# A token tile of the down product behind every second gate or up product, in the first feed-forward of a two-layer model

## The reference

```
xn      = layernorm(x)                                    # 2048 tokens x 512
w_gu    = fp4_values(gate_up_packed) * scales             # 2816 x 512, a scale per 128 inputs
w_down  = fp4_values(down_packed) * scales                # 512 x 1408, a scale per 128 inputs
gate,up = split(xn @ w_gu.T)                              # 1408 columns each
h       = silu(gate) * up
y       = h @ w_down.T
x       = x + tanh(g_ffn[0]) * y / sqrt(mean(y*y) + eps)
```

## Time and profile before

| | |
|---|---|
| median of three runs | 2760.99 us |
| the profiled execution, its own time | 2759.97 us |
| its span | 2757.9 us |
| PE busy | 2507.7 us (91%) |
| DVE busy | 1779.6 us (65%) |
| ACT busy | 1390.4 us (50%) |
| POOL busy | 1033.5 us (37%) |
| 508 to 862 us: PE, DVE, ACT, POOL busy | 316.8, 272.0, 202.5, 190.6 of 354 us |
| granted clock of PE over the span | 0.961 of full speed |

### The profile page before, as it was taken

The page is one execution under the profiler, slowest core; times in us unless marked ns, Lnnn a source line. Parts: engine busy times, 40 slices in busy tenths (PEclk is TensorE's granted clock), DMA queues, the critical chain, the costliest instruction groups (busy, mean ns, idle before and its releaser), DMA issues. The chain is left out here.

```text
span 2757.9 us, 46086 instructions
## 1 busy us (share of the span) xinstructions
PE 2507.7 (91%) x15884; PEld 1965.6 (71%) x15884; DVE 1779.6 (65%) x3774; ACT 1390.4 (50%) x3499; POOL 1033.5 (37%) x965
## 2 busy tenths in 40 slices
PE   7899997699997999998999999999999997299994
PEld 4666664467765788886888888888888886155552
DVE  6767698687876666665766666666667664622221
ACT  4777876455654444443655555555555553022221
POOL 3344321455554555554322222222222221055552
PEclk9999999899998999998999999999999998599997
DMA  3110121200103555557512522331141127599997
GB/s 138 50 47 22 44 65 49 86 1 31 54 31 117 196 181 185 198 178 249 163 47 65 158 74 63 113 97 43 55 151 52 44 78 240 165 301 298 298 297 164
DMA packets 220906, 337.05 MB, mean 122 GB/s; under 512 B 23556, under 2 KB 104836, under 8 KB 220164
## 3 DMA queue, kind: packets, MB, share of 16 engines
q1 hardware_dynamic: 203363, 290.70, 33.2%
q0 software_dynamic: 14912, 39.85, 6.3%
q10 hardware_dynamic: 2400, 3.55, 0.4%
HBM read 227.70 MB, written 110.53 MB: 123 GB/s over the span
## 5 line engine op out<-in xcount | busy, mean ns | idle before, releaser
L2150 POOL TENSOR_SCALAR a_prob<-a_prob,a_rinv 128x640 f32<-128x640 f32 (+3 forms) x256 | 253.7, 991 | 743.0 <-DVE a_rinv L2312 743.0
L2302 DVE TENSOR_REDUCE a_mx<-a_s_ps 128x1 f32<-128x640 f32 (+3 forms) x256 | 262.3, 1024 | 250.1 <-PE a_s_ps L2222 244.8
L2174 ACT ACTIVATE a_probT<-a_t_ps 128x512 fp32r<-128x512 f32 (+3 forms) x512 | 237.2, 515 | 350.1 <-PE a_t_ps L2230 350.1
L2318 DVE TENSOR_TENSOR a_probT<-a_t_ps,a_probT 128x512 fp32r<-128x512 f32 (+3 forms) x512 | 276.7, 582 | 44.7 <-ACT a_probT L2174 44.1
L2165 ACT ACTIVATE a_prob<-a_s_ps,a_nb,a_rs 128x640 f32<-128x640 f32 (+3 forms) x256 | 268.0, 1047 | 9.7 <-DVE a_nb L2303 9.7
L137 PE MATMUL a_o_ps<-a_probT,a_v 128*128 128x256 f32 x832 | 244.4, 294 | 0.0
L138 PE MATMUL a_o_ps<-a_probT,a_v 128*128 128x256 f32 x832 | 232.7, 280 | 0.0
L139 PE MATMUL a_o_ps<-a_probT,a_v 128*128 128x256 f32 x832 | 232.3, 279 | 0.0
L2230 PE MATMUL a_t_ps<-kept_ident,a_prob 128*128 128x128 f32 x1664 | 225.3, 274 | 2.6 <-POOL a_prob L2150 2.6
L2230 PEld LDWEIGHTS a_t_ps<-kept_ident,a_prob 128*128 128x128 f32 x1664 | 194.4, 141 | 25.7 <-POOL a_prob L2150 3.3
L716 PE MATMUL a_bank<-kept_ident,a_prob 128*128 128x128 f32 x1024 | 162.8, 288 | 41.7 <-ACT a_prob L574 31.3
(11 more groups left out here) (318 smaller groups left out, 6822.1 us busy)
## 6 DMA issues: line engine op xcount, KB each, us to landing
expert_ring<-in_w_gate SPq DMA_DIRECT2D x64, 384.0 KB, 19.2
expert_ring<-in_w_up SPq DMA_DIRECT2D x64, 384.0 KB, 21.3
expert_ring<-in_w_down SPq DMA_DIRECT2D x64, 384.0 KB, 24.3
l_q_hi<-p_turned SPq DMA_DIRECT2D x64, 256.0 KB, 2.4
l_q_lo<-p_turned SPq DMA_DIRECT2D x64, 256.0 KB, 2.1
h_split<-l_q_hi SPq DMA_DIRECT2D x62, 256.0 KB, 3.2
h_split<-l_q_lo SPq DMA_DIRECT2D x62, 256.0 KB, 3.8
l_v_hi<-p_vs SPq DMA_DIRECT2D x32, 256.0 KB, 2.3
```

The lines of the kernel that those rows point to most:

```text
L2150: pool.tensor_scalar(prob[:, k % 4, 0:w], prob[:, k % 4, 0:w], rinv[:, k % 4:k % 4 + 1], 1.0, ALU.mult, ALU.mult).then_inc(s["weighted"], 1)
L2174: act.activation(probT[0][:, pair % 2, i * 4:i * 4 + n, k % 2], t_ps[i][:, 0:n * P].rearrange("p (m n) -> p m n", n=P), ACT.Copy).then_inc ...
L2302: step(dve.tensor_reduce(mx[:, k % 4:k % 4 + 1], s_ps[:, k % 2, 0:w], AX.X, ALU.max))
L2318: dve.tensor_tensor(probT[1][:, pair % 2, i * 4:i * 4 + n, k % 2], t_ps[i][:, 0:n * P].rearrange("p (m n) -> p m n", n=P), probT[0][:, pai ...
```

## The change

No instruction is added or removed; the order of each engine's list changes, and with it what each wait stands in front of.

- PE: the down product of step k - 2 is no longer one piece behind `up(k)`: after the jobs 1, 3, 5, 7 stands token tile 0, 1, 2, 3 of it. In the steps with turned tiles these now come behind the whole down product, directly in front of the next `up`.
- ACT: tanh of k - 1 stands behind evict 0, high of k - 1 behind evict 4; copies and squares stand behind evict 6.
- DVE: the gate value of k - 1 (one half of `make`) stands behind evict 1, the rest of `make` behind evict 3.
- POOL: in iteration k first both adds of k - 1, then low of k - 1; rms and root stand behind that low.

```diff
@@ POOL
                 for k in range(1, STEPS0 + 1):
                     u, i = k // IC, k % IC
-                    if k >= 2:
-                        low(k - 2)
                     add(k - 1, 0)
                     add(k - 1, 1)
+                    low(k - 1)
                     if k < STEPS0 and u and i == 3:
                         rms(u - 1, slice(0, SUB))
                     if k < STEPS0 and i == 8:
                         ffn["root"](pool, u + 1)
-                low(STEPS0 - 1)
@@ ACT
-                    for r in (0, 2, 4, 6):
-                        evict(k, r)
+                    evict(k, 0)
+                    if k:
+                        tanh(k - 1)
+                    evict(k, 2)
+                    evict(k, 4)
+                    if k:
+                        high(k - 1)
+                    evict(k, 6)
                     for job in turned_behind(k):
                         turned_high(*job)
-                    if k:
-                        tanh(k - 1)
                     if u and i == 1:
                         copy_y(u - 1, 0)
                         copy_y(u - 1, 1)
                     if u and i == 2:
                         for t in range(SUB):
                             square(u - 1, t)
-                    if k:
-                        high(k - 1)
@@ PE, in up(k)
                         pe.matmul(bank_of(job)[:], w, xT[u % 2][0][:, a], start=False, stop=True).then_inc(s["job_done"], 1)
-
-                def down(k):
+                        if r % 2:
+                            down(k - LAG0, (r // 2,))
+
+                def down(k, tiles=range(SUB)):
@@ PE, in down(k)
-                    for t in range(SUB):
+                    for t in tiles:
@@ PE, the loop
                     up(k)
                     for job in turned_behind(k):
                         turn(*job)
-                    down(k - LAG0)
                 down(STEPS0 - 2)
                 down(STEPS0 - 1)
@@ DVE
-                def make(k):
+                def gate_value(k):
                     dve.wait_ge(s["tanhed"], k + 1)
                     step(dve.scalar_tensor_tensor(th[:, k % 2], th[:, k % 2], 1.0, total[:, k % 3, 0], ALU.add, ALU.mult))
+
+                def make(k):
                     dve.wait_ge(s["summed"], 2 * k + 2)
@@ DVE, the loop
                     for r in (1, 3, 5, 7):
                         evict(k, r)
+                        if k and r == 1:
+                            gate_value(k - 1)
+                        if k and r == 3:
+                            make(k - 1)
                         if r == 1 and u and i == 3:
                             mean(u - 1, slice(0, SUB), u * SUB)
                     for job in turned_behind(k):
                         turned_low(*job)
-                    if k:
-                        make(k - 1)
@@ DVE, after the loop
+                gate_value(STEPS0 - 1)
                 make(STEPS0 - 1)
```

## The result

The changed kernel takes 2780.38 us (median of five runs, 2773.61 to 2781.14) against 2764.67 (2758.08 to 2767.07) for the kernel before: ratio 1.0055, interval 1.0038 to 1.0071. It is slower, by more than 0.3% (the whole interval lies above it). The profiled execution took 2780.38, its span 2778.3, 20.4 us over the span before. The page's totals say little: PE is still busy for 91%.

A forecast was written before the change was run, and what follows sets the result against it. PE was taken to bound the plain steps already, with about 50 us of excess, mostly in special stretches, as the ceiling. Terms summed to -1.0 us from 2759.97, so 2759 us, with 8 in 10 between 2749 and 2771.

The forecast's parts named there:

- The plain step: Steps without special work stay bound by PE and lose small gaps, 6.66 to 6.53 us: -2.0 us over sixteen.
- h's loop: Rival: the loop making h, 6.07 us, passes 6.53 and bounds the steps, tile 0 waiting for low; 2771, chance 0.18.
- The wait in front of a new unit: At k = 11, 22, 33 PE waits 1.75 us for turned tiles, no product covering it: +5.3 us.
- The pow behind low: GpSimd's pow at i = 3, now behind low, ends at T+8.9, making VectorE wait before its adds.
- PE's wait at i = 9: Root behind low delays four normalise instructions at i = 8, so PE waits 2.8 us in the next step.
- k = 10's wait for down_low: At k = 10 the down product waits for down_low(4), behind the turned tiles on VectorE: 2.2 us late.
- (d): Norm of the unit before, at i = 2 to 4: squares, pow and adds come later, +0.7 us.
- (e): Statistics and normalisation at i = 6 to 9: +0.4 us for two units; unit 0's k 7 to 10, +1.7 us.
- clock rival: New waits drop PE's clock, 1.5 us per fall, five falls beyond the layout: +7.5 us, 2766; chance 0.12.
- (a): Next stage's weights at k 38 and 42: k 39's loss falls from 6.2 to 2.7 us, -3.5.
- (b): The end, step 43: last product at T+14.65 instead of 18.65, -4.0 us.
- (f): The start, k 0 to 2: tanh(0) blocks ScalarE's evict 2 until the first add, +0.4 us.

The follow-up runs named there:

- experiments 7: The changed kernel with GpSimd's two adds per step over 64 of 512 columns (does not compute the reference): 2738.74 us, ratio 0.9917 to the kernel before.
- experiment 8: The kernel before with GpSimd's adds cut to 64 of 512 columns (other sums left out): 2750.12 us, ratio 0.9955 to the kernel before.
- experiment 1: The changed kernel with GpSimd's two pow instructions (i = 3 and i = 8) ahead of low again: 2771.26 us, ratio 1.0030 to the kernel before.
- experiment 2: The changed kernel with the last two down-product tiles behind the turned tiles at i = 9 and 10: 2774.97 us, ratio 1.0044 to the kernel before.
- experiment 9: The changed kernel with pow ahead of low and VectorE's side work mostly one unsplit block behind make: 2770.76 us, ratio 1.0027 to the kernel before.

## Why the prediction was wrong

**Right.** The plain step: laid out at 6.53, measured 6.51, with the gate, make, high and low within 0.1 of their places; h's loop did not become the bound (tile 0 waits 0.25 to 0.28 for L1232 at k 4, 5, 7 and 43, and in no plain step). The wait in front of a new unit, which the old profile did not show:

```profile
780.85 1.03 PE L1346 MATMUL f_bank<-kept_ident,f_yx 128*128 128x128 f32 x8
...
782.12 1.29 DVE L1406 TENSOR_TENSOR f_xT<-f_bank,f_xT 128x512 fp32r<-128x512 f32 x2 [0.63 <-ACT f_xT L1258]
...
783.51 0.48 PE L1365 MATMUL f_bank<-f_xT,h_split 128*128 128x512 f32 x1 [1.62 <-ACT f_xT L1258]
```

1.62, three times, against 1.75 predicted. The row names ScalarE, whose pair ended at 782.57; VectorE's L1406 ended at 783.41, 0.10 before PE went on, so the wait is for VectorE, as forecast. The pow behind low and VectorE idle on it; PE's wait at i = 9 of 2.48 against 2.8; k = 10's wait for down_low, 2.79 against 2.2.

**Wrong, the step that failed.** "The price of this order is that VectorE's extra work ... now starts at T+7.14". In the paragraph before it, the layout has GpSimd's next add begin at T+6.56. The two numbers were never laid on each other: no piece of side work was given more than its row of before, where most lay in GpSimd's pause. shift_bits, mask_bits, scale_bits and the 128x4 multiplication had rows of 0.75, 0.69, 1.22 and 0.22 and took 1.80, 1.67, 2.37 (beside an add) and 1.18. The pieces whose rows had met GpSimd before (the first two scaled adds at 2.46, now 2.52, and the four normalisations at 3.85) kept their lengths. k 3 to 6, which the prediction counted as plain steps, lost 3.4 us by it, and short adds gave all of it back (experiments 7 and 8); at k 7 to 10 it acts too, with a fall of the clock behind each of two waits. In (d) it gives 1.0 a unit by L1472 and, at i = 5, two scaled adds of 3.55 us; PE waits 1.41 behind these in unit 1, 0.98 before. The loss of (e) in units 1 and 2 is another: the wait at i = 9 was in the layout, and 2.8 of the 4.9 us are two falls of the clock; the rest is not traced to a cause.

The Trainium skill (SBUF — State Buffer, "Who interferes with whom") was quoted in the prediction for the gate value alone. For a VectorE instruction in a mode that takes both of its SBUF ports, which it says tensor_scalar can enter, the section has it that "whoever issues first gets the shared pair for the whole instruction". The trace agrees: L1472, a tensor_scalar, takes 1.19 us instead of 0.22 and ends with the add. A list of VectorE's instructions of these two kinds (two inputs in SBUF, or tensor_scalar in SBUF) against GpSimd's would have found the long ones above; the gate value, which the prediction priced by it, was the smallest case (0.69 to 0.78 on average).

**Wrong, a size.** The clock rival had its price right (1.5 a fall; seven matmuls x 0.197 = 1.4) and was given 0.12. The slow groups went from five to eleven. Held against it was that three stretches with waits up to 1.86 stood at 1.00; but the layout's own waits at i = 9 and k = 10 were 2.8 and 2.2, longer than any wait in those stretches. In the changed kernel slow matmuls followed eleven of the twelve waits of 2.06 us and more (not that of k = 15), before, five of six, and in experiment 1 no wait of 1.85 or less. No single length parts them, though: in experiment 2 four of eleven such waits (2.57, 2.52, 2.17 and 2.16) went without, and in experiment 9 slow matmuls followed waits of 1.85, 1.98 and 2.00 and not one of 2.45. Why a given wait lowered the clock stays open. At i = 9 it costs its 1.4 a unit. At i = 4 it is nearly free: unit 1 without it took 24.83 and unit 2 with it 24.80, since PE at full clock then waits 1.41 at i = 5 instead. The Trainium skill (TensorE: Matmul & The Clock Gate, "A second HAM failure mode: psum-queue depth-cycling") speaks of frequent short idles; in the kernels before and changed the waits under 2 us left the clock alone, and single long ones were followed by its fall. In experiment 8 eight slow matmuls at k = 43 stand behind two waits of 1.02 and 1.18 us, 1.9 apart, which is nearer to what the page describes.

(a) and (b) gained little more than half of their sums for the first reason: the pair of subtractions took 4.39 beside the adds, not 3.70, and the adds 3.52, so that evict 7 of step 43 came at T+10.4, not 8.6. k 39 also kept eight slow matmuls of twelve (clock 0.84, not free of the fall as forecast). (f): tanh(0) held evict 2 back as said, and nine more matmuls than before ran slow, 1.8 us of the 2.1.

## What to carry to other kernels

When work is moved to another time, its duration moves with its neighbours: before summing, write the VectorE instructions that work in SBUF alone and GpSimd's instructions of the new order on one time line, and give every overlap the rest of the other's instruction, unless a row shows that kind unharmed, as the statistics here. An instruction of four columns can be held as long as a wide one. Put VectorE's side work in GpSimd's pause and in pieces that fit between two evictions. A wait of PE that grows to the length at which the same trace shows slow matmuls can cost a second time, here 1.4 us.

## What was not expected of the hardware

A VectorE instruction of 4 columns, 0.22 us alone, took 1.18 to 1.30 behind a GpSimd add of 1.27. GpSimd pays as well: in the changed kernel pairs of adds of 2.53 took 2.97 to 3.63 beside VectorE's 1024-column work, and in the kernel before 4.48 at k = 39. Evictions that read PSUM stayed at 0.75 in every kernel. Adds of 64 columns instead of 512 saved three times as much in one order of the same instructions as in the other.
